# Second and fourth cross attention of a perceiver: scores in 64 by 64 tiles over interleaved key rows

## The reference

```python
def _L1_xattn_ref(queries, keys, values, mask, ...):       # l1x
    Q, K, V = ...                                          # 16 heads of 16 features
    scores = jnp.einsum('bhqd,bhkd->bhqk', Q, K) / scale
    scores = jnp.where(mask, scores, NEG_INF)              # a mask for each batch
    attention = jax.nn.softmax(scores, axis=-1)
    heads_out = jnp.einsum('bhqk,bhkd->bhqd', attention, V)
    return heads_out... @ W_proj.T + b_proj

def _L3_xattn_ref(x, y, attn_bias, ...):                   # l3x
    q = _l2norm(q) * scale_mul
    k = _l2norm(k)
    attn = jnp.einsum('bhqd,bhkd->bhqk', q, k) + attn_bias # one bias for all batches
    attn = jax.nn.softmax(attn, axis=-1)
    return ... @ Wo + bo
```

## Time and profile before

| what | us |
|---|---|
| median of 3 runs | 2486.48 |
| the profiled execution, whole | 2501.07 |
| its span | 2499.3 |
| PE busy (89% of the span) | 2236.3 |
| DVE busy (66%) | 1650.0 |
| ACT busy (50%) | 1243.2 |
| POOL busy (32%) | 808.3 |

### The profile page before, as it was taken

One profiled execution on the slowest core, in us unless ns is written; L12 is line 12 of the kernel. 1 busy time (PEld: TensorE's weight loads), 2 busy tenths in 40 slices (PEclk: granted clock), 3 DMA queues, 4 the chain that ended last, 5 costly groups with the idle time before them and its releaser, 6 DMA issues. The chain is left out here.

```text
span 2499.3 us, 50978 instructions
## 1 busy us (share of the span) xinstructions
PE 2236.3 (89%) x20593; PEld 1417.7 (57%) x20650; DVE 1650.0 (66%) x3182; ACT 1243.2 (50%) x2071; POOL 808.3 (32%) x660
## 2 busy tenths in 40 slices
PE   6885779999978889999999999699879999998898
PEld 4764445666654555656655666356546555566554
DVE  4987456555548756888888854644576666665577
ACT  2326234555554225555555554566436555563565
POOL 5610052233206112321233300045445455433254
PEclk8998899999989989999999999899999999999999
DMA  3200453423313047676776764133322323220231
GB/s 113 71 7 1 144 136 103 107 78 106 79 66 106 13 118 144 121 133 133 151 146 122 125 113 80 34 102 102 116 67 67 86 69 86 69 67 23 71 96 60
DMA packets 358618, 226.84 MB, mean 91 GB/s; under 512 B 289913, under 2 KB 326610, under 8 KB 358386
## 3 DMA queue, kind: packets, MB, share of 16 engines
q1 hardware_dynamic: 355314, 215.20, 35.5%
q0 software_dynamic: 3072, 8.39, 1.2%
HBM read 114.87 MB, written 0.52 MB: 46 GB/s over the span
## 5 line engine op out<-in xcount | busy, mean ns | idle before, releaser
L3950 POOL TENSOR_TENSOR l2x_rows<-l2x_rows,l2x_one 128x256 f16<-128x256 f32 (+1 forms) x91 | 89.2, 1006 | 379.6 <-DVE l2x_rows L1507 354.5
L100 PE MATMUL PS<-hot 128*128 128x512 f16 x460 | 134.3, 427 | 82.1 <-DVE l0a_g L1119 17.5
L4054 PE MATMUL PS<-l2x_rows,l2x_pth 128*128 128x512 f16 x832 | 200.3, 379 | 1.7 <-DVE l2x_mean L4263 1.7
L3711 DVE CUSTOM_DVE_ANT_0 l1x_junk<-PS,l1x_bias 128x1024 bf16<-128x1024 f32 (+1 forms) x128 | 123.2, 991 | 73.6 <-PE PS L3371 72.7
L4256 DVE TENSOR_TENSOR l2x_pl<-l2x_sc,l2x_ph 128x1664 f16<-128x1664 f32 x64 | 125.1, 1954 | 44.6 <-ACT l2x_ph L4133 43.9
L4151 ACT ACTIVATE l2x_meanT<-PS 128x256 f32<-128x256 f32 x64 | 24.5, 383 | 250.5 <-PE PS L4016 250.5
L4241 DVE CUSTOM_DVE_ANT_0 l2x_sc<-PS,l2x_bias 128x1665 f32<-128x1665 f32 x64 | 120.9, 1889 | 36.3 <-issue 35.0
L3711 DVE CUSTOM_DVE_ANT_0 l3x_junk<-PS,l3x_bias 128x1024 bf16<-128x1024 f32 (+1 forms) x128 | 123.6, 991 | 24.3 <-PE PS L3371 21.6
L4008 PE MATMUL PS<-l2x_kh,l2x_qth 128*128 128x512 f16 (+1 forms) x512 | 131.9, 339 | 1.5 <-issue 1.5
L4008 PE MATMUL PS<-l2x_kh,l2x_qtl 128*128 128x512 f16 (+1 forms) x512 | 131.9, 339 | 0.0
L4008 PE MATMUL PS<-l2x_kl,l2x_qth 128*128 128x512 f16 (+1 forms) x512 | 131.9, 339 | 0.0
(11 more groups left out here) (866 smaller groups left out, 6109.0 us busy)
## 6 DMA issues: line engine op xcount, KB each, us to landing
l2f_unit<-in_L_ffn_units_dram SPq DMA_DIRECT2D x36, 384.0 KB, 3.1
l3f_unit<-in_L_ffn_units_dram SPq DMA_DIRECT2D x34, 384.0 KB, 3.0
l1x_kst<-l1x_kh SPq DMA_DIRECT2D x128, 100.1 KB, 2.2
l3x_kst<-l3x_kh SPq DMA_DIRECT2D x128, 100.1 KB, 2.2
l2x_rows<-in_ctx_dram SPq DMA_DIRECT2D x8, 1536.0 KB
l1x_ctx<-in_ctx_t_dram SPq DMA_DIRECT2D x7, 1601.0 KB, 7.3
l3x_ctx<-in_ctx_t_dram SPq DMA_DIRECT2D x7, 1601.0 KB, 7.0
l1x_kst<-l1x_kl SPq DMA_DIRECT2D x64, 100.1 KB, 2.2
```

The costliest lines, as they stand in the source:

```text
L100: self.nc.tensor.matmul(self.PS[:, bank, :], self.hot[:, 0:P], self.hot[:], start=True, stop=True)
L3711: v.tensor_tensor_reduce(junk[:, slot(it), 0:n], slot_banks(it)[:, 0:n], bias[:, 0 if normed else b % 2, at:at + n], 1.0, LOWEST, ALU.add, ...
L3950: last = nc.gpsimd.tensor_tensor(high[:, at], of[:, at], one[0:p, at].unsqueeze(2).unsqueeze(3).to_broadcast([p, i, NC, P]), ALU.mult)
L4054: nc.tensor.matmul(PS[:, ACC, :], pth[:, u % 2, m, :], rows2[:, b % 2, :, :, m, :], start=(m == 0), stop=False)
```

## The change

The contraction becomes 64 rows to a head and the score tiles become 64 by 64.

- Rows. `kst` has 128 rows: head r of the pair (r = 0, 1) takes the partitions 64 r to 64 r + 63, and in them feature d of part x lies at 4 d + x. Part 0 is constant (it carries the maximum against the first of the 16 rows in `qst`, the others are zero there), the parts 1 to 3 are the three products. `stack` still makes 24 transfers of 32 partitions, two heads each, now to every fourth partition. `qst` loses the second copy of its columns: 64 columns for a head.
- A items. Two pairs and a quarter of the keys (401 columns, the last 398): four matmuls, each 64 rows of contraction by 64 queries, one to each quarter of the array; head r goes to bank r of the slot, pair i to output rows 64 i. Still 16 items. DVE takes the maximum in two operations of 401 columns an item.
- Transposed scores. `turned(b, m)` makes both halves at once: bank r takes the heads r of all 8 pairs, in 32 matmuls of 64 by 64 by 64 columns. It waits for both exponentials of the part before, and in part 0 for both M items of the batch. The mask on PE is four matmuls of 512 columns in l1x; in l3x its high and low part no longer fit into one contraction, so it is eight.
- l1x adds its mask on PE in all 13 parts (`ON_VECTOR` empty); `bias_t`, `mask_t` and their transfers and conversions go. l3x keeps the parts 0 to 3 on DVE.
- M items are two transposes instead of four, and two copies of 256 on ACT instead of one of 512.
- ACT and DVE: first both exponentials (additions of the mask) of the part, then the items of both its steps; `step_before` goes.
- Preparation: the queries are split and turned in float16 (`q3` in 3 operations instead of 4, one matmul for each turn instead of a float32 transpose), their copies out of PSUM halve in number; the constant rows are filled by two transfers of 32 partitions by 8 by 1601.

```diff
-    ON_VECTOR = list(range(4))
+    ON_VECTOR = list(range(4)) if normed else []
-    A = [("A", u, h) for u in range(R) for h in range(NH)]
+    A = [("A", v, j) for v in range(QV) for j in range(NCH)]
...
-                 [("M", 0, 0), A[10]], [A[11]], [A[12]], [A[13]], [A[14]], [A[15]], [], [("M", 1, 0)]]
+                 [("M", 0, 0), A[10]], [A[11]], [A[12]], [A[13]], [A[14]], [A[15]], [("M", 1, 0)], []]
...
-        kst = sb("kst", [3 * F + 1, 2, R, NK], F16)
+        kst = sb("kst", [P, 2, R, NK], F16)
...
+                sp.wait_ge(const_made, 1)
+                for a in range(2):
+                    sp.dma_start(kst[0::PARTS, a, :, :], const.unsqueeze(1).to_broadcast([F, R, NK])).then_inc(const_rows, 16)
...
-                        for g, part in enumerate((kh, kl, kh)):
-                            sp.dma_start(kst[g * F:(g + 1) * F, b % 2, c * RC + j, :],
+                        for x, part in ((1, kh), (2, kl), (3, kh)):
+                            sp.dma_start(kst[x::PARTS, b % 2, c * RC + j, :],
                                          part[j * F:(j + 1) * F, c, :]).then_inc(stacked[c * RC + j], 16)
...
                     elif kind == "A":
...
-                        for i, at, n in pieces(*halves[j]):
-                            last = nc.tensor.matmul(PS[:, bank + i, 0:n], qst[0:3 * F, b, c, :, :],
-                                                    kst[0:3 * F, b % 2, c, at:at + n], start=True, stop=True)
+                        at, n = chunks[j]
+                        for i in range(2):
+                            for r in range(2):
+                                rows = slice(r * S, (r + 1) * S)
+                                last = nc.tensor.matmul(PS[i * S:(i + 1) * S, bank + r, 0:n], qst[rows, b, 2 * c + i, :],
+                                                        kst[rows, b % 2, 2 * c + i, at:at + n], start=True, stop=True)
...
-                def turned(b, m, g):
+                def turned(b, m):
...
-                            pe.wait_ge(exp_done, e - G2 + 1)
+                            pe.wait_ge(exp_done, e)
                     if m == 0:
-                        pe.wait_ge(row_made, G2 * b + g + 1)
+                        pe.wait_ge(row_made, G2 * (b + 1))
...
+                    for u in range(R):
+                        for at, w_ in keys:
+                            for r in range(2):
+                                rows = slice(r * S, (r + 1) * S)
+                                last = nc.tensor.matmul(PS[at:at + w_, S_BANK + r, u * S:(u + 1) * S],
+                                                        kst[rows, b % 2, u, m * P + at:m * P + at + w_], qst[rows, b, u, :],
+                                                        start=not on_tensor, stop=not on_tensor or u == R - 1, skip_group_check=True)
...
                     for m in range(KT):
+                        turned(b, m)
                         for g in range(G2):
-                            turned(b, m, g)
                             for it in at_step(b, m * G2 + g):
                                 item(it)
...
                         for g in range(G2):              # ACT; DVE alike
-                            for it in step_before(b, m * G2 + g):
+                            exp(b, m, g)
+                        for g in range(G2):
+                            for it in at_step(b, m * G2 + g):
                                 item(it)
-                            exp(b, m, g)
...
+                        for r in range(2):               # DVE, an A item
+                            last = v.tensor_tensor_reduce(junk[:, slot(it), r * BANK:r * BANK + n], PS[:, 2 * slot(it) + r, 0:n],
+                                                          bias[:, 0 if normed else b % 2, at:at + n], 1.0, LOWEST, ALU.add, ALU.max,
+                                                          rmax[:, r, c, j:j + 1])
```

More of the change, by code:

```diff
@@ L2996, in context_attention @@
     G2 = 2
-    UG = R // G2
+    PARTS = 4
+    QCOLS = PARTS * DH
+    CHUNK = -(-NK // 4)
+    chunks = [(at, min(CHUNK, NK - at)) for at in range(0, NK, CHUNK)]
+    NCH = len(chunks)
+    QV = R // 2
     VW = DH + 1
     Q4 = P // 4
-    HG = H // G2
     VT = 4
@@ L3036, in context_attention @@
     assert len(steps) == STEPS
-    WARM = (3, 2)
+    WARM = 3
     OFF_SLOT = "IUQTRFZY"
@@ L3411, in turned @@
                     on_tensor = m not in ON_VECTOR
+                    keys = [(at, min(S, n - at)) for at in range(0, n, S)]
                     if on_tensor:
-                        of_bias = fsp[:, m * P:m * P + n] if normed else bias[:, b % 2, m * P:m * P + n]
-                        nc.tensor.matmul(PS[0:n, S_BANK + g, :], of_bias, one_hot[:], start=True, stop=False)
-                    for i in range(UG):
-                        u = g * UG + i
-                        last = nc.tensor.matmul(PS[0:n, S_BANK + g, i * P:(i + 1) * P], kst[:, b % 2, u, m * P:m * P + n],
-                                                qst[:, b, u, :, :], start=not on_tensor,
-                                                stop=not on_tensor or i == UG - 1)
@@ L3420, in turned @@
-                    last.then_inc(turned_made, 1)
+                        for x in range(2 if normed else 1):
+                            for at, w_ in keys:
+                                for r in range(2):
+                                    half = slice(r * S, (r + 1) * S)
+                                    of_bias = fsp[half, x, :] if normed else bias[half, b % 2, :]
+                                    nc.tensor.matmul(PS[at:at + w_, S_BANK + r, :], of_bias[:, m * P + at:m * P + at + w_], one_hot[half, :],
+                                                     start=(x == 0), stop=False, skip_group_check=True)
@@ new lines, in turned @@
+                    for u in range(R):
+                        for at, w_ in keys:
+                            for r in range(2):
[3 more added lines that the diff above has]
+                                                        start=not on_tensor, stop=not on_tensor or u == R - 1, skip_group_check=True)
+                                if u == R - 1 and at == keys[-1][0]:
+                                    last.then_inc(turned_made, 1)
@@ L3429, in values @@
                         pe.wait_ge(v_read, b * NV + m // VT + 1)
-                    for i in range(HG):
-                        h = g * HG + i
-                        at = (h % 4) * Q4
-                        last = nc.tensor.matmul(PS[at:at + VW, PV_BANK + b % 2, (h // 4) * S:(h // 4 + 1) * S],
-                                                v33[0:n, b % 2, m, h, :], pT[0:n, (b * KT + m) % 2, g, i * S:(i + 1) * S],
-                                                start=(m == 0 and h < 4), stop=(m == KT - 1), skip_group_check=True)
+                    for u in range(R):
+                        at = (u % 4) * Q4
+                        block = 2 * g + u // 4
+                        last = nc.tensor.matmul(PS[at:at + VW, PV_BANK + b % 2, block * S:(block + 1) * S],
+                                                v33[0:n, b % 2, m, 2 * u + g, :], pT[0:n, (b * KT + m) % 2, g, u * S:(u + 1) * S],
+                                                start=(m == 0 and block == 0), stop=(m == KT - 1), skip_group_check=True)
                     last.then_inc(summed, 1)
```

158 lines of the change are left out of this document (72 added, 86 removed).

## The result

The changed kernel takes 2591.8 us (median of 4 runs, 2586.07 to 2599.96), the kernel before on the same chip 2487.64: a ratio of 1.0414 (95% interval 1.0376 to 1.0452). It is slower by 104 us, where no change was forecast, and far outside the range. The profiled execution took 2586.07.

What follows compares the result with a forecast made beforehand. PE, busy 93%, was taken to bound both layers. In us, l1x batches -7, last batches +4.1 and +6, preparations -3 and -2, l3x batches +1 summed to about -1: 2485, no change; range 2455 to 2515.

Steps and rivals of the forecast that it cites:

- PE's gain: Change on PE alone: 5.1 us a batch less in l1x, 4.2 in l3x, 65 over 14 batches, most not arriving.
- The round of four quarters: Four 64 by 64 tiles at a time on PE: taken as 0.033 us a round.
- the first rival: Array quarters don't run four at a time: 2558 us, or 2510 with only weight loads in turn; chance 0.13.
- transposed scores of a part: 8 rounds, 0.26: PE, each part's score block: 0.26 us for 2 x 0.22, 0.18 less, 2.3 a batch.
- The chain through ACT: Next scores wait for both exponentials: part at least 1.87 us (l1x), 2.09 (l3x); last batches +4.1 and +6.0.
- l1x, a batch: l1x batch without O and P: 44.8 us for 45.7, -1.0, seven times -7.
- its own sign of being wrong: Prediction wrong if a last-batch part takes under 1.8 us, or an l1x batch under 43.5 or over 46.
- l3x, a batch: l3x batch, 53.5 us before: 1.9 gained in parts 0 to 5, 2.0 lost later; +0.1, seven times +1.
- A8 now needing two pairs of key rows from SP instead of one (3 transfers of 0.62): l3x, parts 6 to 12: put at 0.8 us a batch together with the M item behind both exponentials.
- The pairing of the exponentials costs more: Slots freed only behind both exponentials: 1.2 us more a batch, 2502; slower once an l3x batch passes 54.5; chance 0.17.
- The gain arrives: Waits shorter than counted, half of PE's 65 us arrives: 33 us, 2452; chance 0.27.
- Preparations and the mask: Preparations: l1x -3 us, l3x -2. Mask on PE: l1x 1.0 a batch less, l3x as before.

Runs made afterwards that it cites:

- e1_grouped: Changed kernel with only part 12's matmuls reordered, all tiles of one key first, then all of 64, masks too; 2548.2 us, 1.0249 of the kernel before.
- e4_split: As e1_grouped, transposed scores and mask made bank by bank, each behind its own exponential, two tiles side by side; 1.0547 of the kernel before.
- e9_max_dve: As e1_grouped, with the two copies of an M item on DVE in place of ACT; 1.0196 of the kernel before.
- e7_early: As e1_grouped, in l3x four of the six transfers that A8 waits for start once the high part is there; 1.0187 of the kernel before.
- e6_filled: As e1_grouped, with 12 unread matmuls of 512 columns on PE ahead of item A8 of l3x; 1.0184 of the kernel before.
- e14_wide_repaired: e1_grouped, e6_filled (8 matmuls), e7_early and e9_max_dve together, with the wide tiles of e13_wide_mixed in both layers; 1.0072 of the kernel before.
- e13_wide_mixed: As e11_mixed_dve, l1x's transposed scores and mask in tiles of 64 rows by all keys of a part; 2481.6 us, 0.9971 of the kernel before.
- e12_mask_pe: Kernel before, with only l1x's mask of parts 0 to 3 moved to PE too; 1.0040 of the kernel before.
- e11_mixed_dve: As e8_mixed, with the copies of the M items on DVE in l1x; 1.0018 of the kernel before.
- e8_mixed: l3x as before; l1x as e1_grouped, last batch bank by bank, ACT's items between the exponentials in parts 8 and 9; 1.0003 of the kernel before.

## Why the prediction was wrong

*PE's gain.* The round of four quarters was right (0.032 us, for 0.033), and with it the end of the first rival: the scores of a part of 128 keys take 0.25 to 0.35 at 2.4 GHz, not 0.5. The step that failed is its first line, "transposed scores of a part: 8 rounds, 0.26", taken times 13. The thirteenth part has a tile of one key beside each of 64, and each change of width costs 0.14 towards the narrow tile and 0.12 back: mask and scores take 2.78 for 0.60 in l1x and 4.41 for about 0.8 in l3x, in 16 batches. I had priced changes of shape at 0.09 between blocks and did not look for them inside one. Together with what it drew after it, this is 41 of the 104 us (e1_grouped).

*The chain through ACT.* Right to 0.02: 1.86 a part for 1.87 in l1x and 2.07 for 2.09 in l3x, and e4_split brings 1.54 back. But for part 12, which with the end took 5.2 and 5.9 for 3.2 and 3.4, the last batches would have been 25.6, as forecast, and 28.8: in l3x the parts 0 to 3, with the mask on DVE, took 8.8 together for 7.5.

*l1x, a batch.* Summed at 44.8 for a batch without O and P; the changed kernel took 46.8 to 49.5, over the 46 that the prediction gave as its own sign of being wrong. With part 12's excess of 1.5 gone, in e1_grouped, it takes 45.2: parts 4, 6 and 7 took 8.15 (8.1), part 5 5.6 (5.6), parts 8 and 9 6.8 (7.0), parts 10 to 12 7.1 (6.7). The error is in part 12, where the second M's copies stand behind both exponentials and the next part 0 needs them. e9_max_dve gets 0.4 of it back there.

*l3x, a batch.* This is where the sum broke: +0.1 forecast, +6 even in e1_grouped. The step was "A8 now needing two pairs of key rows from SP instead of one (3 transfers of 0.62)", put into 0.8 with the M item. It named the right wait and sized it as if other work stood between. But from POOL's last split to the next batch everything is one chain: rows, eight A items of about 1.0 on DVE, M, part 0. A8 came 2.2 later against the first transfer (5.9 for 3.7), since the sixth transfer is issued 3.3 to 4.4 behind the first and lands 2.3 to 3.1 after that, and nothing behind it could give way. e7_early, which only starts transfers sooner, gains 15 us, e9_max_dve 13 in both layers.

*The clock.* It had no term at all. I counted waits as their own length. l3x had 97 us at 1.2 GHz: grouping part 12 took 22 of them away (e1_grouped), and filling the wait for the key rows, up to 4.0 us a batch, with matmuls that nobody reads took another 51, which gained 16 us (e6_filled).

*The rivals.* "The pairing of the exponentials costs more", 2502, came nearest: slots freed late are real, but they are 13 us of it, and its point, a batch of l3x over 54.5, was passed mainly by the key rows and part 12. "The gain arrives" is shown wrong for these tiles: with every wait that I found repaired, e14_wide_repaired is 1% behind e13_wide_mixed, and 18 of these 25 us are l3x (488 us long for 470). What of that is DVE's 16 items in two operations each and what the paired slots was not measured apart.

*Preparations and the mask.* Summed at -3 and -2. From the layer's first matmul to its first scores l1x took 52.6 for 53.2, and l3x 76.0 for 70.6: -0.6 and +5.5, and in e1_grouped l3x still has +4.3. No run takes these terms apart. l1x's mask on PE alone costs 10 us in the kernel before (e12_mask_pe); in the changed one parts 0 to 3 still fell to 17.3, as forecast (17.4).

## What to carry to other kernels

Price the remainder tile by itself: a loop that alternates full and narrow tiles pays for each change of width, and grouping them cost nothing here. A wait that is short beside a batch is not small if it lies on the chain that hands one batch to the next, and if PE is the engine that stands still it may be paid twice, in the wait and in the clock behind it. Before cutting matmuls into smaller ones, count instructions a us: halves of the array did the same work as quarters with fewer instructions, and only with them did the change to l1x become a gain. And a transfer that is issued earlier has not landed earlier: compare landings.

## What the runs showed of the hardware

- Alternating tiles of 64 and of 1 output row cost 0.27 us for a group of four matmuls of 64 columns (2.14 for eight groups, 658.07 to 660.21): 0.14 to 0.15 from 64 to 1 and 0.12 back. The groups of one shape cost 0.032. What PE does in a change is not shown.
- PE halts for its instructions: in the last batch of l1x the halts of e11_mixed_dve are 256 instructions and 3.5 to 4.0 us apart, one transfer of instructions before each. Over eight parts PE was given 71 a us in two kernels with different parts (137 and 105 instructions), 67 and 69 in e1_grouped and e8_mixed, 74 in e4_split. The transfers are 16.4 KB each (3.49 MB in 213). The Trainium skill (Advanced Engine Details and Errata, section "ISA Cache") gives lines of 16 KB that hold 256 instructions; the size of the transfers agrees, and the count between the halts too.
- A round of 512 columns with 64 rows of contraction took as long with four tiles of 64 output rows (0.25 to the next block, 714.12 on) as with one of 128 (0.23, 694.98 on).
